# Routed experts of a six-stage network: new slots for the router's work, logits with both weight parts in one stationary operand, inverse roots by bits on VectorE, the next stage's statistics in the tail

## The chip, the cores and the metric

The kernel runs on one core of one Trainium2 chip. The metric is the time of one execution on the device in microseconds; the median of three runs is compared. Engines are named as in the profile: PE is TensorE, DVE is VectorE, ACT is ScalarE, POOL is GpSimd, SP is SyncE.

## The reference, cut to what matters

The network has six stages on `x` of (4, 1024, 256), 4096 tokens of 256 numbers:

```python
x = x + 0.5 * ffn0(layernorm(x))      # call 0: routed experts
x = x + attn0(layernorm(x))           # call 1
x = x + 0.5 * ffn0(layernorm(x))      # call 2: the same experts again
x = x + 0.5 * ffn1(layernorm(x))      # call 3
x = x + attn1(layernorm(x))           # call 4
x = x + 0.5 * ffn1(layernorm(x))      # call 5
```

The routed experts, `ffn0`, are:

```python
h = layernorm(x) * g + b              # of the normalised x: two norms in a row
logits = h @ Wr                       # (4096, 7)
top_vals, top_idx = top_k(logits, 2); gates = softmax(top_vals)
pos = place of each (token, choice) in its expert, in order; keep = pos < 732
xe[expert, pos] = h[token]
ye = (silu(xe @ W1) * (xe @ W3)) @ W2           # per expert, 256 -> 1024 -> 256
routed[token] += gate * keep * ye[expert, pos]
shared = (silu(h @ W1s) * (h @ W3s)) @ W2s      # every token
out = routed + shared
```

732 is the capacity of an expert (`CAP0`).

## The kernel before, in words

`x` stays in SBUF as `X`, 32 tiles of 128 tokens. Each stage is a class (`Ffn0`, `Attn0`, `Ffn1`, `Attn1`) with one ordered list of items. Every engine goes through the same list and issues what it has to do of each item (methods `pe`, `act`, `dve`, `pool`, `sp`), so the list sets the order on each queue, and semaphores carry what depends on what. Between stages stands a barrier, the item `meet`.

**A routed call (`Ffn0`).** Each product is made in three matmuls of fp32r parts (`mm3`, lines 160 to 162): high x high, low x high, high x low. The shared FFN of all tokens is `units` 0 to 3 of 8 steps each; unit 3 has one of its two halves here and the other at the very end. The seven experts are the units between. A step `s` is: `up(s, h)` for each half `h` (two banks of 12 matmuls altogether, Silu on ACT at line 502, product on DVE at 587, high part on ACT at 506, low part on DVE at 590), then `down(s - 1)`, and in every other step the load `ld` (SP, lines 860 to 862) and the split `wt` of the next weights (ACT 512, DVE 595). All shared steps work on banks 0 to 2 and 4 to 7; the router's work shares bank 3 and one buffer `AUX`.

**The router's work is put into slots** between the pieces of the first 24 steps, three slots to a step: slot `3s` is behind `up(s, 0)`, `3s + 1` behind `up(s, 1)`, `3s + 2` at the step's end. The items are: `stats` (mean and variance of tiles, lines 177 and 180), `root` (inverse root of the variance), `norm` (line 214, writes the normalised tiles `Z`), `tp(h, c)` (four transposes of a group of 512 tokens at line 457, gain and bias on ACT at 535, high part at 545, low part on DVE at 621), `lg(h)` (logits of 512 tokens, eight matmuls at line 474, read by ACT at 551), `lt(h)` (four small transposes of them at 481, copied by DVE at 626), `best` (the two largest of each token, 632 and 636), `tot` (one-hot table at 640 and 644, totals over all tokens at 484, a copy at 650), `pos` (method `positions`, the row number of each token and choice, with Exp on ACT for the gates), and `scat` (GpSimd, line 794).

Before, tiles 0 to 7 get all of this ahead of step 0, one part in a row, and the split of the first weights is last. Groups 2 to 7 have `tp` from slots 13, 17, ... 33; `tot` is in slot 38, `pos` in 39.

**The scatter.** 64 indirect DMAs write rows of 272 numbers of `Z` to memory `xe_scratch`, 32 for each choice; column 256 is the gate, 257 the token. Behind the first 32, GpSimd waits for them to land (the item `("scat", n, 4)`), copies the second choice's gate into column 256 (line 791) and issues the other 32. It then reads the rows of experts 0 and 1 (`xr`, line 804). TensorE asks for expert 0's rows in unit 3 of the shared FFN (`xt`, line 464), in step 26:

```python
elif ui == 3 and 2 <= j < 6:
    sl[2] = [("xt", n, 0, j - 2)] + ([("gi", n, 0)] if j == 5 else [])
```

**The roots.** `Ffn0.root` makes two roots in a row, as there are two norms: `Sqrt` on ACT (line 518), then a reciprocal and a Newton step on DVE, twice; the variance of the second norm is worked out from the first. The other stages take `Ln` and `Exp` on ACT (lines 209 and 211) and two Newton steps of four DVE instructions each (lines 197 to 203). ACT holds one set of tables at a time: Silu, Sqrt and Exp each need a load (`ACT_TABLE_LOAD`).

**Tails.** In the last unit `xget` reads X back from memory, since the experts' results were added there; the last sums into X are at line 661. Then `meet`, then the next stage begins with its statistics.

Of the kernel before, what the change touches and what calls it, by code (L numbers as in the profile page):

```python
# [16 lines left out]
LOW, HIGH = 16512, 229344  # L17

# [78 lines left out]
class Chip:  # L97
# [4 lines left out]
    def __init__(self, nc, A, out, ctx):  # L102
# [9 lines left out]
        self.S1, self.S2, self.S3, self.S4 = (self.sm(NT) for _ in range(4))  # L112
# [70 lines left out]
    def root_var(self, e, w, gs):  # L183
        w.wait_ge(*self.p.mine())
        e.tensor_scalar(self.S1[:, gs], self.MV[:, gs, 1], 1e-5, None, ALU.add).then_inc(*self.p.one("ln_var"))

    def root_dve(self, e, w, gs, it, by=None):
# [4 lines left out]
        if not by:  # L192
            self.root_var(e, w, gs)
        w.wait_ge(*p.at("ln_root", by or it))
        for n in range(2):
            i_ = o if n else s2
            e.tensor_tensor(s3, i_, i_, ALU.mult).then_inc(*p.one("dv"))
# [3 lines left out]
            e.tensor_scalar(s3, s3, -0.5, 1.5, ALU.mult, ALU.add).then_inc(*p.one("dv"))  # L201
            w.wait_ge(*p.mine())
            e.tensor_tensor(o, i_, s3, ALU.mult).then_inc(*p.one("rt" if n else "dv"))
            w.wait_ge(*p.mine())

    def root_act(self, e, w, gs, it, by=None):
        p = self.p
        w.wait_ge(*p.at("ln_var", by or it))
        e.activation(self.S2[:, gs], self.S1[:, gs], ACT.Ln).then_inc(*p.one("ac"))
        w.wait_ge(*p.mine())  # L210
        e.activation(self.S2[:, gs], self.S2[:, gs], ACT.Exp, scale=-0.5).then_inc(*p.one("ln_root"))
# [20 lines left out]
class Ffn0:  # L232
# [9 lines left out]
        "root": {}, "norm": {"z": 1},  # L242
# [7 lines left out]
    def __init__(self, chip, call, first):  # L250
# [23 lines left out]
        self.GI, self.IF6 = [c.sm(6) for k in range(2)], c.sm(12)  # L274
# [20 lines left out]
        for it in self.items:  # L295
# [3 lines left out]
            if it[0] == "root" and it[3] < 2:  # L299
                counts = {"ln_var": 1, "ln_root": 1}  # L300
# [10 lines left out]
            p.count(it, counts)  # L311
        c.back = {b: (self.back(2 * b), ("xget", call, min(2 * b + 1, 6))) for b in range(4)}
# [3069 lines left out]
```

## Time and profile before

| what | us |
|---|---|
| median of three runs | 3152.45 (3150.3 to 3153.19) |
| the profiled execution's own time | 3148.64 |
| its span | 3146.8 |
| PE busy | 2809.8 (89%) |
| DVE busy | 1821.0 (58%) |
| ACT busy | 1644.4 (52%) |
| POOL busy | 610.2 (19%) |

The profiled execution's own time is 1.84 us over its span. Times in rows are us from the span's start; the clock is the share of 2.4 GHz that was granted to PE, so 0.50 is the lower level of 1.2 GHz. Call 0 goes from 0 to 738 us, the first attention to 1107, call 2 to 1831. Matmuls overlap, so a busy PE is not a PE at its peak.

### The profile page before, as it was taken

The page shows a single profiled execution, that of the slowest core. Times are in us where ns is not written, and L with a number is a line of the kernel's source. Part 1 is how long each engine was busy: PE and PEld are TensorE (multiplying, and loading weights), DVE is VectorE, ACT ScalarE, POOL GpSimd, SP SyncE. Part 2 cuts the span into 40 slices and gives each one's busy share as a digit, 9 for nine tenths or more (in the row PEclk, how much of TensorE's full clock was granted, in tenths as well). Part 3 has the DMA queues.
Part 4 walks back from the last instruction along what each step waited for, and adds up shares of the span by engine and source line. Part 5 has one row for each costly group of instructions (what it writes and reads, how often), then busy time and mean ns, then how long its engine had stood idle before and what let it go on. Part 6 is the DMA issues. An engine that isn't in the chain of part 4 may idle for free.

```text
span 3146.8 us, 53051 instructions
## 1 busy us (share of the span) xinstructions
PE 2809.8 (89%) x21463; PEld 2169.0 (69%) x21463; DVE 1821.0 (58%) x3719; ACT 1644.4 (52%) x2535; POOL 610.2 (19%) x555
## 2 busy tenths in 40 slices
PE   6898999997999968989999945897899999993998
PEld 4677999995666656779999935796333434332898
DVE  5554555546777665545555467786635364326786
ACT  3433455543443434335555433564687778891665
POOL 0026021212000000360212254633000000001343
PEclk9999999998999989999999977998999999995999
DMA  3224243323000021232433344574442243413675
GB/s 130 89 69 131 87 100 83 85 70 87 2 2 2 2 51 44 90 121 78 100 81 94 77 133 130 152 196 109 101 121 46 65 105 96 80 34 115 169 192 129
DMA packets 240643, 287.20 MB, mean 91 GB/s; under 512 B 30916, under 2 KB 218492, under 8 KB 240400
## 3 DMA queue, kind: packets, MB, share of 16 engines
q1 hardware_dynamic: 201856, 223.88, 24.8%
q0 software_dynamic: 34848, 56.28, 9.0%
q8 instruction: 169, 2.77, 0.4%
q10 hardware_dynamic: 3696, 3.67, 0.4%
q14 instruction: 74, 0.61, 0.1%
HBM read 204.72 MB, written 87.93 MB: 93 GB/s over the span
## 4 chain that ended last, share of the span: by engine, by line
PE 63%; DVE 12%; issue 8%; POOL 7%; ACT 5%; DMA 4%; SPq 0%; POOLq 0%; DVEq 0%; ACTq 0%
PE PS L2842 14%; PE PS L160 12%; PE PS L161 11%; PE PS L162 11%; PE PS L1001 9%; POOL xe_scratch L794 4%; POOL xa_scratch L2295 1%; ACT FW L512 1%; PE PS L474 1%; DVE SM L177 1%; DVE FW L595 1%; DMA GR<-xn_scratch,SM 1%; POOL GR L2280 1%; ACT Z L561 1%; DVE PROD L587 1%
## 5 line engine op out<-in xcount | busy, mean ns | idle before, releaser
L2991 ACT ACTIVATE P<-PS 128x1024 f32<-128x1024 f32 x512 | 487.9, 1035 | 106.4 <-PE PS L2842 104.1
L160 PE MATMUL PS<-FH,FW 128*128 128x366 f32 (+1 forms) x1408 | 512.7, 364 | 26.4 <-DVE FW L595 13.5
L161 PE MATMUL PS<-FH,FW 128*128 128x366 f32 (+1 forms) x1408 | 502.9, 357 | 0.0
L162 PE MATMUL PS<-FH,FW 128*128 128x366 f32 (+1 forms) x1408 | 499.9, 355 | 0.0
L506 ACT ACTIVATE FHH<-PROD 128x366 fp32r<-128x366 f32 (+1 forms) x352 | 195.3, 555 | 487.0 <-DVE PROD L587 487.0
L160 PE MATMUL PS<-FW,FHH 128*122 128x256 f32 (+1 forms) x1184 | 339.4, 287 | 1.5 <-DVE FHH L590 1.5
L587 DVE TENSOR_TENSOR PROD<-SIL,PS 128x366 f32<-128x366 f32 (+1 forms) x352 | 207.0, 588 | 226.1 <-PE PS L162 215.6
L590 DVE TENSOR_TENSOR FHH<-PROD,FHH 128x366 fp32r<-128x366 f32 (+1 forms) x352 | 210.0, 596 | 218.6 <-ACT FHH L506 218.6
L161 PE MATMUL PS<-FW,FHH 128*122 128x256 f32 (+1 forms) x1184 | 335.3, 283 | 0.0
L162 PE MATMUL PS<-FW,FHH 128*122 128x256 f32 (+1 forms) x1184 | 334.5, 283 | 0.0
L160 PEld LDWEIGHTS PS<-FH,FW 128*128 128x128 f32 x1408 | 268.4, 191 | 54.8 <-ACT SIL L502 14.8
L162 PEld LDWEIGHTS PS<-FH,FW 128*128 128x128 f32 x1408 | 269.5, 191 | 22.7
L161 PEld LDWEIGHTS PS<-FH,FW 128*128 128x128 f32 x1408 | 268.2, 191 | 19.5 <-issue 1.5
L2842 PE MATMUL PS<-P,V 128*32 128x512 f32 x2048 | 273.3, 606 | 1.9 <-DVE OC L3138 1.4
L812 POOL DMA_INDIRECT xa_scratch<-Z,SM x84 | 140.9, 1677 | 615.1 <-ACT Z L561 593.7
L595 DVE TENSOR_TENSOR FW<-WST,FW 128x1536 fp32r<-128x1536 f32 x96 | 168.7, 1757 | 148.1 <-ACT FW L512 148.1
L502 ACT ACTIVATE SIL<-PS 128x366 f32<-128x366 f32 (+1 forms) x352 | 180.9, 514 | 127.8 <-PE PS L162 127.2
L794 POOL DMA_INDIRECT xe_scratch<-Z,SM x128 | 146.9, 1148 | 440.9 <-DVE SM L760 401.5
L160 PEld LDWEIGHTS PS<-FW,FHH 128*122 128x122 f32 (+1 forms) x1184 | 222.9, 188 | 5.7 <-DVE FHH L590 1.9
L161 PEld LDWEIGHTS PS<-FW,FHH 128*122 128x122 f32 (+1 forms) x1184 | 222.8, 188 | 2.7
L162 PEld LDWEIGHTS PS<-FW,FHH 128*122 128x122 f32 (+1 forms) x1184 | 222.6, 188 | 0.0
L2842 PE MATMUL PS<-S,S 64*128 64x512 f32 x1024 | 195.2, 454 | 1.4 <-DVE S L3132 1.0
(446 smaller groups left out, 5446.4 us busy)
## 6 DMA issues: line engine op xcount, KB each, us to landing
WS<-L_ffn_w_dram SPq DMA_DIRECT2D x256, 256.0 KB, 3.8
WST<-L_ffn_W_dram SPq DMA_DIRECT2D x168, 256.0 KB, 3.6
S<-parts_scratch SPq DMA_DIRECT2D x60, 384.0 KB, 7.9
parts_scratch<-PT SPq DMA_DIRECT2D x28, 512.0 KB, 4.4
Z<-xe_scratch POOLq DMA_DIRECT2D x14, 777.8 KB, 8.5
WST<-L_ffn_W1s_dram SPq DMA_DIRECT2D x40, 256.0 KB, 2.9
WST<-L_ffn_W3s_dram SPq DMA_DIRECT2D x40, 256.0 KB, 3.6
WST<-L_ffn_W2s_dram SPq DMA_DIRECT2D x40, 256.0 KB, 4.2
```

Of the source, the lines that this page charges most:

```text
L160: e.matmul(o, lh, rh, start=start, stop=False, skip_group_check=True)
L161: e.matmul(o, ll, rh, start=False, stop=False, skip_group_check=True)
L162: return e.matmul(o, lh, rl, start=False, stop=stop, skip_group_check=True)
L502: e.activation(self.SIL[:, h, 0:NH], c.bank(2 * self.up_at[it] % 3, NH), ACT.Silu).then_inc(*p.one("sil"))
L506: e.activation(self.FHH[:, s % 2, 0, hs], self.PROD[:, h, 0:NH], ACT.Copy).then_inc(*p.one("hi"))
L587: e.tensor_tensor(self.PROD[:, h, 0:NH], self.SIL[:, h, 0:NH], c.bank((2 * self.up_at[it] + 1) % 3, NH), ALU.mult).then_inc(*p.one("mul"))
L590: e.tensor_tensor(self.FHH[:, s % 2, 1, hs], self.PROD[:, h, 0:NH], self.FHH[:, s % 2, 0, hs].bitcast(F32), ALU.subtract).then_inc(*p.one( ...
L595: e.tensor_tensor(self.FW[:, q % 2, 1, :], self.WST[:, q % 2, :], self.FW[:, q % 2, 0, :].bitcast(F32), ALU.subtract).then_inc(*p.one("wo"))
L794: e.indirect_dma_start(out=c.XE, out_offset=bass.IndirectOffsetOnAxis(ap=c.ROWS.bitcast(U32)[:, m:m + 1], axis=0), in_=self.Z[:, m % NT, : ...
L1001: mm = lambda o, l, r, a=True, z=True: e.matmul(o, l, r, start=a, stop=z, skip_group_check=True)
L2842: mm = lambda o, l, r, a=True, z=True: e.matmul(o, l, r, start=a, stop=z, skip_group_check=True)
L2991: e.activation(self.PR[K % 3][:, 2 * jj:2 * jj + 2, :].rearrange("p a b -> p (a b)"), c.pair(2 * ((2 * K + jj) % 3)), ACT.Exp, scale=0.25) ...
```

## The change

Slots: the split of the first weights (`wt 0`) goes ahead of the first transposes, and the split of the router's weights gets an item of its own (`wrr`) behind the norms, so that statistics wait for neither. The groups' `tp` begin at slots 7, 11, ... 27; the one-hot table becomes an item `oh` in slot 32, `tot` is in 33, `pos` in 34, `scat` in 35 to 42, the reads of rows in 44.

```diff
-        seq += [("stats", n, 0, 0, 4), ("stats", n, 0, 4, 8)] + [("root", n, 0, k) for k in range(3)]
-        seq += [("norm", n, i, i + 4) for i in (0, 4)] + [("tp", n, h, c) for h in range(2) for c in range(2)]
-        seq += [("wt", n, 0)]
+        self.ahead = [[("stats", n, 0, 4)], [("stats", n, 4, 8)]]
+        seq = [("consts", n), ("ld", n, 0), ("ld", n, 1), *self.ahead[0], *self.ahead[1], ("root", n, 0, 8)]
+        seq += [("norm", n, i, i + 4) for i in (0, 4)] + [("wrr", n), ("wt", n, 0)]
+        seq += [("tp", n, h, c) for h in range(2) for c in range(2)]
...
-            slots[k].append(it)
-        for k in range(8):
-            slots[k].append(("stats", n, 1 + 3 * k // 8, 8 + 3 * k, 11 + 3 * k))
-        for k in range(3):
-            slots[8 + k].append(("root", n, 1, k))
-        for k in range(12):
-            slots[11 + k].append(("norm", n, 8 + 2 * k, 10 + 2 * k))
+            slots[k + k // 4].append(it)
+        for k, a, b in ((0, 8, 11), (1, 11, 14), (2, 14, 16), (4, 16, 18), (5, 18, 20), (7, 20, 23), (8, 23, 26),
+                        (9, 26, 29), (10, 29, 32)):
+            slots[k].append(("stats", n, a, b))
+        slots[3].append(("root", n, 8, 16))
+        slots[11].append(("root", n, 16, 32))
         for h in range(2, 8):
-            s0 = 13 + 4 * (h - 2)
+            s0 = 7 + 4 * (h - 2)
+            for k in range(2):
+                slots[s0 - 3 + k].append(("norm", n, 4 * h + 2 * k, 4 * h + 2 * k + 2))
...
-        slots[38].append(("tot", n))
-        slots[39].append(("pos", n))
+        slots[32].append(("oh", n))
+        slots[33].append(("tot", n))
+        slots[34].append(("pos", n))
         for k in range(8):
-            slots[40 + k].append(("scat", n, k))
-        slots[48] += [("xr", n, 0), ("xr", n, 1), ("xput", n, 7)]
+            slots[35 + k].append(("scat", n, k))
+        slots[44] += [("xr", n, 0), ("xr", n, 1), ("xput", n, 7)]
```

Logits: the high and the low part of the router's weights stand side by side in one stationary operand of 16 columns, so a group takes four matmuls, and both halves are summed as they are read from the small transposes.

```diff
-                    for x, y in ((0, 0), (1, 0), (0, 1), (1, 1)):
-                        ins = e.matmul(pb[0:8, :], self.WRR[:, y, cc, :], self.FH[h // 2][:, x, cc, hs],
...
+                    for x in range(2):
+                        ins = e.matmul(pb[0:16, :], self.WRR[:, cc, :, :].rearrange("p y e -> p (y e)"),
+                                       self.FH[h // 2][:, x, cc, hs], start=cc + x == 0, stop=cc + x == 2,
...
-            e.tensor_copy(self.LG[:, 4 * h:4 * h + 4, 0:7],
-                          c.bank(3, 32).rearrange("p (i e) -> p i e", e=8)[:, :, 0:7]).then_inc(*p.one("ad"))
+            e.tensor_reduce(self.LG[:, 4 * h:4 * h + 4, 0:7],
+                            c.bank(3, 64).rearrange("p (i y e) -> p i e y", y=2, e=8)[:, :, 0:7, :], AX,
+                            ALU.add).then_inc(*p.one("ad"))
```

Roots: one function for all stages, twelve DVE instructions, none on ACT. The first guess comes from the number's bits; the double norm of `Ffn0` is one root of `v * (1 + eps) + eps * eps`. In the second attention the items `rv` and `ra` go, and the shift of one `root` stands for them.

```diff
+    def root(self, e, w, gs, done, by=1.0, more=EPS):
...
+        e.tensor_scalar(s1, self.MV[:, gs, 1], by, more, ALU.mult, ALU.add).then_inc(*p.one("dv"))
...
+        e.tensor_scalar(s2, s1.bitcast(U32), -0.5, 1597463007.0, ALU.mult, ALU.add).then_inc(*p.one("dv"))
...
+        e.tensor_copy(o.bitcast(U32), s2).then_inc(*p.one("dv"))
...
+        for n in range(3):
+            e.scalar_tensor_tensor(s3, o, -0.5, o, ALU.mult, ALU.mult).then_inc(*p.one("dv"))
...
             e.tensor_tensor(s3, s3, s1, ALU.mult).then_inc(*p.one("dv"))
...
+            e.scalar_tensor_tensor(o, s3, 1.5, o, ALU.add, ALU.mult).then_inc(*p.one(done if n == 2 else "dv"))
```

Scatter: the row carries both gates and the token's first expert (columns 256, 258, 259), and the reader takes the gate that belongs to its expert: four DVE instructions in `gi` for two. The wait and the copy between the two halves go.

```diff
-            if it[2] == 4:
-                w.wait_ge(*p.at("scat", ("scat", n, 3)))
-                w.wait_ge(*p.mine())
-                e.tensor_copy(self.Z[:, :, D], c.GT[:, 1, :]).then_inc(*p.one("po"))
-                w.wait_ge(*p.mine())
...
+        e.tensor_copy(self.Z[:, :, D + 2], c.GT[:, 1, :]).then_inc(*p.one("dv"))
+        e.tensor_copy(self.Z[:, :, D + 3], self.IF[:, 0, :]).then_inc(*p.one("dv"))
```

Tails: `joined` moves a stage's first items into the list of the stage before. A routed call takes the first attention's two pairs of statistics ahead of its last `up`, and their root ahead of its last sums; the first attention takes call 2's two pieces of statistics ahead of `("lc", 1, 3, 0, 0)` and `("le", 1, 3, 3)`, near its end. `Ffn1` and `Attn1` neither give nor take.

```diff
+def joined(ph, after):
+
+    pieces = after.ahead if after and ph.rooms else ()
+    out, at = [], 0
+    for room, piece in zip(ph.rooms, pieces):
+        out += [(ph, ph.items[at:room]), (after, piece)]
+        at = room
+    out.append((ph, ph.items[at:]))
...
+        self.rooms = [self.items.index(it) for it in (self.ups[-1], ("xs", call, len(self.units) - 1))]
...
+        self.ahead = [self.items[1:3], self.items[3:4]]
+        self.rooms = [self.items.index(("lc", call, 3, 0, 0)), self.items.index(("le", call, 3, 3))]
```

## Rows read from the trace of the kernel before

**Rows 1.** The chain that ended last, its summary by line (share of the span).

```profile
by line: PE PS L2842 13.7%; PE PS L160 12.1%; PE PS L161 11.3%; PE PS L162 11.3%; PE PS L1001 8.9%; issue 8.2%; POOL xe_scratch L794 3.7%; POOL xa_scratch L2295 1.3%; ACT FW L512 1.1%; PE PS L474 1.0%; DVE SM L177 1.0%; DVE FW L595 0.9%; DM
```

**Rows 2.** Windows, call 0: stretch, length, busy us (x instructions) per engine, PEclk, DMA share, GB/s.

```profile
28.50:77.50 49.00, 43.91 (x212) 35.08 (x213) 30.94 (x109) 19.73 (x27) 0.00 (x0) 0.92 0.23 79
77.50:189.20 111.70, 98.09 (x533) 76.54 (x532) 56.18 (x158) 47.33 (x70) 0.00 (x0) 0.94 0.21 71
189.20:209.10 19.90, 15.57 (x65) 11.91 (x66) 12.62 (x36) 4.89 (x7) 0.00 (x1) 0.83 0.21 66
209.10:303.70 94.60, 94.60 (x550) 83.61 (x550) 46.28 (x60) 35.73 (x53) 72.13 (x64) 1.00 0.35 115
```

**Rows 3.** The same view, call 2; engines in the order PE, PEld, DVE, ACT, POOL.

```profile
1131.00:1180.00 49.00, 43.94 (x213) 35.11 (x214) 31.03 (x110) 19.73 (x27) 0.00 (x0) 0.92 0.22 49
1180.00:1286.00 106.00, 93.67 (x533) 74.65 (x531) 56.42 (x158) 47.32 (x70) 0.00 (x0) 0.98 0.13 40
1286.00:1305.00 19.00, 15.07 (x66) 11.64 (x67) 12.21 (x36) 5.01 (x7) 0.21 (x1) 0.91 0.22 71
1305.00:1400.00 95.00, 94.91 (x552) 83.79 (x550) 46.39 (x61) 36.03 (x53) 73.27 (x65) 1.00 0.35 117
1400.00:1412.50 12.50, 0.14 (x1) 0.17 (x2) 2.35 (x2) 1.48 (x1) 1.24 (x3) 0.57 0.84 232
```

**Rows 4.** Waits of PE, 0 to 720 us: us in total, times, longest.

```profile
PE PS L464 <- DMA Z<-xe_scratch: 13.7, 1, 13.7
PE PS L474 <- DVE FH L621: 8.4, 6, 3.2
...
PE PS L160 <- ACT SIL L502: 5.1, 7, 2.9
PE PS L484 <- DVE RT L644: 4.6, 1, 4.6
```

**Rows 5.** Timeline, start of call 0: start us, us, instruction, idle before.

```profile
9.71 1.40 DVE L177 BATCH_NORM_STATS2 SM<-X 128x6 f32<-128x256 f32 x4
...
13.49 0.17 DVE L710 TENSOR_SCALAR SM<-SM 128x8 f32<-128x8 f32 x1
...
17.22 2.80 DVE L214 TENSOR_SCALAR Z<-X,SM 128x256 f32<-128x256 f32 x8
...
28.52 0.80 PE L160 MATMUL PS<-FH,FW 128*128 128x512 f32 x1 [6.12 <-DVE FW L595]
```

**Rows 6.** DMA issues of 0 to 4.7 us: KB each, median us to landing.

```profile
X<-L_attn_x_dram SPq DMA_DIRECT2D x1, 512.0 KB, 5.0
...
WST<-L_ffn_W2s_dram SPq DMA_DIRECT2D x1, 256.0 KB, 9.8
```

**Rows 7.** Call 2: DMA issues of 1107 to 1110.2 us; then the timeline's first matmul.

```profile
WST<-L_ffn_W2s_dram SPq DMA_DIRECT2D x1, 256.0 KB, 4.4
...
1130.97 0.80 PE L160 MATMUL PS<-FH,FW 128*128 128x512 f32 x1 [6.12 <-DVE FW L595]
```

**Rows 8.** Groups of instructions (busy us, mean ns, idle before), from call 0.

```profile
L474 PE MATMUL PS<-FH,WRR 128*8 128x512 f32 x64 | 19.0, 446 | 10.6 <-DVE FH L621 8.4 <-DVE RT L626 2.1
...
L457 PE MATMUL PS<-IDENT,Z 128*128 128x128 f32 x64 | 11.2, 316 | 22.3 <-DVE Z L214 20.6 <-DVE RT L626 1.7
...
L791 POOL COPY Z<-SM 128x32 f32<-128x32 f32 x1 | 0.2, 243 | 3.1 <-DMA xe_scratch<-Z,SM 3.1
```

**Rows 9.** Groups of instructions, call 0: loads of ACT's tables ahead of Sqrt.

```profile
L518 ACT ACT_TABLE_LOAD x3 | 3.8, 1283 | 9.7 <-issue 9.7
```

**Rows 10.** Timeline, inside the scatter of call 0, DVE and POOL.

```profile
249.76 1.76 DVE L595 TENSOR_TENSOR FW<-WST,FW 128x1536 fp32r<-128x1536 f32 x1 [2.38 <-ACT FW L512]
...
249.84 2.54 POOL L794 DMA_INDIRECT xe_scratch<-Z,SM  x1 [0.30 <-issue]
```

**Rows 11.** Timeline, end of call 0 and start of the attention, DVE.

```profile
736.81 1.29 DVE L661 SCALAR_TENSOR_TENSOR X<-PS,X 128x512 f32<-128x512 f32 x2 [1.79 <-PE PS L162]
...
742.96 0.75 DVE L177 BATCH_NORM_STATS2 SM<-X 128x6 f32<-128x256 f32 x2
```

More of the change, by code:

```diff
@@ L17 @@
 LOW, HIGH = 16512, 229344
+EPS = 1e-5
 class Sig:
@@ L111, in __init__ @@
         self.ST, self.MV, self.R = self.sm(8, 6), self.sm(NT, 2), self.sm(NT)
-        self.S1, self.S2, self.S3, self.S4 = (self.sm(NT) for _ in range(4))
+        self.S1, self.S2, self.S3 = (self.sm(NT) for _ in range(3))
         self.GB = self.sm(2, 2)
@@ L273, in __init__ @@
         self.OUT = c.sm(2)
-        self.GI, self.IF6 = [c.sm(6) for k in range(2)], c.sm(12)
+        self.GI, self.G2, self.IF6 = [c.sm(6) for k in range(2)], c.sm(6), c.sm(12)
         self.IU = [self.IF6[:, 6 * k:6 * k + 6].bitcast(U32) for k in range(2)]
@@ L512, in act @@
             e.activation(self.FW[:, q % 2, 0, :], self.WST[:, q % 2, :], ACT.Copy).then_inc(*p.one("wh"))
-        elif k == "root":
-            g, part = it[2:]
-            if part < 2:
-                gs = slice(8, NT) if g else slice(0, 8)
-                w.wait_ge(*p.at("ln_var", it))
-                e.activation(c.S2[:, gs], c.S1[:, gs], ACT.Sqrt).then_inc(*p.one("ln_root"))
         elif k in ("tp", "xt"):
@@ L1579, in act @@
         kk = 16 * len(self.bs)
-        if k == "root" and not self.apart:
-            c.root_act(e, w, self.columns(it), it)
-        elif k == "ra":
-            c.root_act(e, w, self.columns(it), it, ("rv", *it[1:]))
-        elif k == "sk" and it[3] == 0:
+        if k == "sk" and it[3] == 0:
             s = it[4]
@@ L1611, in dve @@
         elif k == "root":
-            c.root_dve(e, w, self.columns(it), it, self.apart and ("ra", *it[1:]))
-        elif k == "rv":
-            c.root_var(e, w, self.columns(it))
+            c.root(e, w, self.columns(it), "rt")
         elif k == "zn":
@@ L1937 @@
     NW = 64
+    ahead, rooms = (), ()
     CONSTS1 = 7, 11, 15, 19, 20, 21, 22, 23, 24
@@ L2634, in prep @@
             q.add(1, ("stats", n, "p", b, i), ("stats", n, "p", b, i + 1))
-        for delay, k in ((1, "rv"), (2, "ra"), (2, "root")):
-            q.add(delay, (k, n, "p", b))
-        q.add(1, ("zz", n, b, 0))
+        q.add(1, ("root", n, "p", b))
+        q.add(5, ("zz", n, b, 0))
         q.add(1, ("zz", n, b, 1), ("xb", n, b))
@@ L2682, in sink_jobs @@
         last = b == 2
-        for delay, k in ((1, "rv"), (2 - last, "ra"), (2 - last, "root")):
-            q.add(delay, (k, n, b, 0))
+        q.add(1, ("root", n, b, 0))
         job = []
@@ L3288, in sp @@
             self.all_loaded(w)
+def joined(ph, after):
[5 more added lines that the diff above has]
+    out.append((ph, ph.items[at:]))
+    if pieces:
+        moved = {it for piece in pieces for it in piece}
+        after.items = [it for it in after.items if it not in moved]
+    return out
 KINDS = [Ffn0, Attn0, Ffn0, Ffn1, Attn1, Ffn1]
```

129 lines of the change are left out of this document (44 added, 85 removed), and 6 rows, old and new, of the table COUNTS.

## The prediction

> **What bounds the kernel now.** The chain that ended last comes first: five lines of matmuls hold 57% of it, and the scatter of tokens to the experts (line 794), which computes nothing, holds 3.7% by itself [rows 1]. So the stage that scatters is cut into stretches. In both calls the same picture: a start; four steps of the shared FFN; a long router part; a short stretch up to the moment when the row numbers are ready; 95 us in which TensorE is full at a granted clock of 1.00 while GpSimd scatters; and a hole, 12.5 us long in call 2, in which it does nothing [rows 2, 3]. The waits of TensorE in call 0 put the hole at 13.7 us, all of it for the scattered rows, and show three more kinds: 8.4 us in six waits for the halves of the transposed tokens, 4.6 us in one for the one-hot table, and 2.9 us in the longest of those for ScalarE's Silu [rows 4]. In the shared steps the profile's clock is under 1.00, so time is lost there at the lower of the two levels (1.2 GHz) as well.
>
> **The start of each call.** Before, the first shared matmul issues at 28.52, because the weight split stands behind all four transposes on ScalarE and VectorE [rows 5]. Now the split stands ahead of them, and the statistics no longer wait for gate and bias. The last third of the weights is issued at 4.2, near the end of a stretch of 4.7 us, and lands 9.8 later, at 14.0; the first eighth of X, issued with the first DMAs at 0.8, lands 5.0 later, at 5.8 [rows 6]. Statistics of eight tiles took 3.8 us; the root's 17 small instructions 3.73, 0.22 each [rows 5], so twelve take 2.6; the norms 2.8: normalised tiles are ready at 15.0, beside the weights' copy (14.0 to 15.5) and subtraction (to 17.3). Two subtractions of transposed halves follow, taken as 0.8 each (a third of the weights' 1.76 for a third of the columns is 0.6, the rest for ScalarE's copy): first matmul at 18.9, 9.6 us earlier. In call 2 the statistics are already done in the attention's tail; the weights, issued at 1109.8, land 4.4 later, at 1114.2 [rows 7], and the same 5 us behind them give 1119.2 for 1130.97: 11.8 us. Bounds: 6 and 13 us, as the landing of the weights moves.
>
> **Logits.** Line 474 took 19.0 us for 64 matmuls, 8 per group [rows 8], 2.4 us a group with those at the lower clock; I take 2.0 at the full one. Half of them go, 1.0 us per group. That a stationary of 16 columns costs more than one of 8 is not in the trace; weight loads there lie beside matmuls of 512 columns, so nothing to 0.1 us each, and I take nothing. The summing read of 16 columns in place of a copy I bound by 0 and 0.3 us per group and take nothing: VectorE only, beside TensorE's next matmuls.
>
> **The first four steps** (slots 0 to 11). TensorE was busy 43.9 of 49.0 us [rows 2]. The new slots put in a third logits group (1.0), three transposes (11.2 us for 16 groups, 0.7 each [rows 8]) and 0.4 for a small transpose, less 2 x 1.0 for the halved groups: +1.5. They bring one more wait of 8.4/6 = 1.4. The 2.9 us wait goes: it stands behind the switch of tables from Sqrt back to Silu (1283 ns a switch [rows 9]), and with it about 1.7 of the 3.9 us that a clock of 0.92 lost. 49.0 + 1.5 + 1.4 - 2.9 - 1.7 = 47.3. VectorE is near the same: 30.9 busy, plus 1.5 for two roots, 2.2 for three pairs of norms and 2.1 for three subtractions is 37, plus 0.7 of idleness behind each of eight products: 43. So little is won here, and bounds are -4 and +6 us.
>
> **The router part** (slots 12 to 37 before, 12 to 31 now). Of 98.1 us busy, 6.7 were lost to a clock of 0.94 and 6.0 go with the logits: 85.4. Twelve transposes, six logits groups, six small ones hold 16.8 of it, so a shared step costs 68.6 / 8.67 = 7.9. Now there are 6.67 steps (52.8) with nine, five and five of those (13.3): 66.1. Idle was 13.6; I keep it by slots, 10.5, and 5 for the clock: 81.6 for 111.7. In call 2 the same with 12.3 idle and a clock of 0.98: 66.1 + 9.5 + 2 = 77.6 for 106.0 [rows 3].
>
> **Up to the row numbers.** 19.9 us before. The one-hot table is now made a slot ahead of the totals, so the 4.6 us go, with the 3.4 that a clock of 0.83 lost; one more half step of 2.6 lies in it. 14.5; in call 2, 19.0 - 4.6 - 1.7 + 2.6 = 15.3. The two added copies (0.2 each) are inside the bound.
>
> **The scatter.** The row numbers come 5 slots, 1 2/3 steps, earlier against TensorE's work, so TensorE now has 94.6 + 1.67 x 7.9 = 107.8 us to do before it asks for the first expert's rows. From the same moment the rows took 94.6 + 13.7 = 108.3 to land; 4.1 of it (3.1 of landing, 0.2 of copy [rows 8], and 0.8 until the next issue) was the second gate's column, which goes: 104.2. So the hole closes with 3.6 us to spare. In call 2 it is 95.0 + 13.2 = 108.2 against 107.5 less 3.1 (a shorter landing by 1), 104.4. That margin is all that hides the scatter; a lack is paid one for one. On GpSimd's queue only the two reads of rows stand behind the 64 issues.
> A scatter issue of 0.98 us took 2.54 when a 1.76 us VectorE subtraction began beside it [rows 10]. The Trainium skill ("SBUF — State Buffer", Who interferes with whom) says the shared port pair is an exclusive lock and its loser blocks; the trace agrees, and by it the scatter's time depends on how many subtractions fall into it. By the rows six do, now as before: the sum stays.
>
> **Sum of the calls.** Call 0: 49.0 + 111.7 + 19.9 + 94.6 + 13.7 = 288.9 before, from the first matmul on; 47.3 + 81.6 + 14.5 + 107.8 = 251.2 now; 37.7 gained, and 9.6. Call 2: 281.5 against 47.3 + 77.6 + 15.3 + 108.2 = 248.4; 33.1, and 11.8. Together 92.2 us. What the clock gives back behind the hole is not counted.
>
> **The tails and the other roots.** Between the last sum into X (ended 738.10) and the third pair's statistics lie 4.86 us [rows 11]; less a barrier, taken as 0.2, 4.7 go. In the tail of the call VectorE idled 1.79 us before that sum; the root of 2.6 fits it but for 0.8. The statistics ahead of it need X's first blocks back from memory; if they are late, the last product waits behind them (bounds 0 and 4). In the attention's own tail two pieces of statistics stand ahead of products and sums: 0 if VectorE waits there anyway, 3.8 if all lies on the path; its last sums wait for TensorE, so I take 0. Two roots at the second attention's start cost 0.2 each more. There the set of tables holds both Ln and Exp, so the roots by bits take no table switch away: that part of the change gains nothing outside the routed calls. 4.7 - 0.8 - 0.4 = 3.5.
> By "ScalarE: Activation LUTs" of the Trainium skill (Table sets) a switch costs about 2.7 us; the trace has 1.283 [rows 9], and the measurement decides. With 2.7 the removed wait would be worth 2.8 us more per call.
>
> **Total.** 92.2 + 3.5 = 95.7 us. The profiled execution took 3148.64, so 3052.9; it stands 3.8 us under the median of the runs (3152.45), so the median should be 3057.
>
> **Rivals.** A: the scatter still ends last. TensorE reaches the rows with only 3.6 us of margin; three collisions more, at 1.5 us each, or a faster router part after the row numbers, bring back 1 to 8 us per call with the clock's fall behind it. For it: the margin is 3% of the stretch. Against: both sides are counted from the same moment. 3057 + 12 = 3069. Chance 0.16.
> B: VectorE bounds the dense slots. Its 43 us of 47 are in order, and each wait of it delays a product that TensorE's next banks need. If the first steps take 6 us more than before and the router part keeps its old pace per slot of 4.3 us (86 for 81.6), each call loses (6 + 1.7) + 4.4 = 12.1 of its gain: 3081. For it: the 43 us counted above. Against: the slots before were filled by half as much and TensorE waited 5 us in 49. Chance 0.18.
> C: slower than before. The clock: it fell wherever TensorE paused. If short pauses now come in every slot and hold it at 1.2 GHz, a step of 7.9 us takes up to 15.8. It decides from the point where 96 us of such work, 12 of the 21 steps up to the row numbers in both calls, runs low; if all 21 do, it loses 166 and the time is 3223. Against: the same work has 0.92 to 0.98 [rows 2, 3]. Chance 0.02.
> D: the slots' order is not what sets the pace, and start and hole are all that comes: 21.4 + 26.2 = 48; 3105. Chance 0.03.
> By "TensorE: Matmul & The Clock Gate" of the Trainium skill (The HAM clock gate), the clock is one of two levels and follows how busy TensorE has been; the trace agrees (the hole's mean is 0.57 [rows 3]), and this is the page beside C.
>
> **How the numbers follow.** Forecast 0.60; A 0.16, B 0.18, D 0.03, C 0.02, no change 0.01. The unknown terms (start 6 to 13, first steps +-5, router part +-8 per call) add to about +-25 round 3057; the range reaches to B on the slow side: 3030 to 3090. About 0.2% (6 us) is what a measurement of this kernel can tell from no change: faster 0.97, same 0.01, slower 0.02.
>
> **What would show it.** First shared matmul near 19 us, and 12 us behind the second routed call's start; line 474 with half its matmuls; no table load for Sqrt; first scatter near 162 us after the start, the 64 issues in one piece of about 92 us; no wait of TensorE for the expert rows; the attention's first transposes 4 us earlier behind the last sum. It would be wrong if a wait for rows of over 5 us stands, if VectorE's busy share in the first four steps nears 1, or if the clock there falls under 0.85.

## The result, and the profile after

The changed kernel took 3069.58 us (median of 4 runs, 3065.97 to 3079.62), the kernel before beside it 3151.38 (3147.87 to 3153.19): a ratio of 0.9747 (0.972 to 0.9773), 82 us less. Forecast were 3057, within 3030 to 3090, and a gain of 95.7. The profiled execution is the slowest of the four, 3079.62 us with a span of 3077.7, 69.1 less than the span of 3146.8 before. Where a difference of some microseconds matters, the second profile of the same kernel (changed_again, below; span 3065.0, 81.8 less) stands beside it.

The windows of the changed kernel, cut at the first shared matmul, the start of the fifth step, the first scatter and the first transposes of the experts' rows. ([rows 2, 3] have their second border 4.5 us later, inside the fifth step; the section on the prediction comes back to this.) Busy us and instructions of PE, PEld, DVE, ACT, POOL; then clock, DMA share, GB/s:

```profile
19.06:66.61 47.55, 39.97 (x204) 31.54 (x205) 35.75 (x120) 19.66 (x29) 0.00 (x0) 0.96 0.24 83
66.61:182.08 115.47, 94.39 (x508) 76.70 (x507) 61.54 (x188) 44.44 (x66) 0.00 (x0) 0.91 0.22 73
182.10:289.00 106.90, 106.90 (x622) 94.55 (x621) 51.99 (x67) 40.96 (x60) 74.83 (x66) 1.00 0.41 130
1095.05:1144.67 49.62, 43.00 (x205) 33.54 (x205) 35.84 (x120) 19.71 (x29) 0.00 (x0) 0.87 0.28 49
1144.67:1240.49 95.82, 88.98 (x508) 73.01 (x507) 61.46 (x188) 44.16 (x66) 0.00 (x1) 1.00 0.14 45
1240.50:1347.50 107.00, 107.00 (x622) 94.59 (x621) 52.07 (x67) 41.00 (x60) 76.19 (x66) 1.00 0.41 128
```

There is no fourth stretch any more: TensorE is full from the first scatter to the experts' rows in both calls, and the holes of 13.7 and 12.5 us are gone. But the middle stretch, router part and row numbers together, takes 115.5 us in call 0 and 95.8 in call 2, for the same work; TensorE idles 21.1 us in the one and 6.8 in the other. Its waits in call 0 say on what (0 to 720 us; total, times, longest):

```profile
PE PS L449 <- DVE Z L205: 14.5, 2, 13.4
PE PS L466 <- DVE FH L609: 11.6, 6, 6.8
PE PS L449 <- DVE RT L614: 11.6, 3, 9.7
...
PE PS L477 <- DVE RT L633: 1.9, 1, 1.9
```

The first is the start. The wait for the one-hot table fell from 4.6 to 1.9, and none is left for the experts' rows [rows 4]. Two single waits are new, 6.8 and 9.7 us. VectorE, named in both, was itself idle ahead of them, in its weight splits, here the sixth (VectorE's timeline):

```profile
140.55 1.76 DVE L583 TENSOR_TENSOR FW<-WST,FW 128x1536 fp32r<-128x1536 f32 x1 [8.29 <-ACT FW L505]
```

Before, the sixth split stood at 140.73: the same moment, though TensorE had started 9.5 us later. What holds it stands on SP's queue (timeline; start, us, issues that ran one behind the other):

```profile
75.29 15.32 SPq L821 DMA_DIRECT2D WST<-L_ffn_W1s_dram  x1
...
95.81 13.04 SPq L795 DMA_DIRECT2D xe_scratch<-RT  x2
108.89 11.34 SPq L821 DMA_DIRECT2D WST<-L_ffn_W1s_dram  x1
120.28 7.04 SPq L822 DMA_DIRECT2D WST<-L_ffn_W3s_dram  x1
```

L795 writes zeros into the experts' scratch, 777.8 KB at a time from 122 partitions, seven times in call 0 and never in call 2; a weight load whose issue takes 0.4 us elsewhere waits 11 and 15 behind it. From 98 to 106 us, where these writes run with no more than the rest of one weight load beside them, the DMA share is 0.13, two engines of 16, at 49 GB/s. So the theory to be tested was: in call 0 the pace is that of SP's queue. Its rivals: the denser slots of VectorE, or the clock (0.91 in that stretch).

Three more readings. The start and the seam between call 0 and the attention came as forecast (first shared matmul; last sum of call 0, statistics, norm):

```profile
19.06 0.77 PE L161 MATMUL PS<-FH,FW 128*128 128x512 f32 x1 [2.02 <-DVE FH L609]
```

```profile
706.10 1.29 DVE L651 SCALAR_TENSOR_TENSOR X<-PS,X 128x512 f32<-128x512 f32 x2
707.53 0.76 DVE L178 BATCH_NORM_STATS2 SM<-X 128x6 f32<-128x256 f32 x2
708.32 0.25 DVE L181 BATCH_NORM_AGGREGATE SM<-SM 128x2 f32<-128x6 f32 x2
708.60 1.88 DVE L205 TENSOR_SCALAR ZBUF<-X,SM 128x256 f32<-128x256 f32 x4
```

From sum to norm it is 2.50 us where it was 7.22. But from that norm to the barrier of call 2 the attention took 375.3 us where it had taken 363.1 (744.03 to 1107.13): it lost 12. A part of that is a fall of the clock some 300 us behind the norm. In all profiles of this study it stands in five of the ten with statistics in this stage's tail and in none of the four without (windows, changed kernel):

```profile
1010.00:1015.00 5.00, 5.00 (x82) 4.55 (x76) 1.47 (x5) 2.11 (x3) 0.00 (x0) 0.50 0.00 0
1015.00:1020.00 5.00, 5.00 (x36) 1.42 (x34) 1.31 (x2) 1.55 (x3) 0.00 (x0) 0.58 0.02 3
```

The rest was the second thing to be tested: statistics for call 2 now stand in the attention's tail, its last piece behind the last sum into X.

### The profile page after: what moved, and what is told of

Same layout as the page of the kernel before. It is cut to its first block, busy times and chain, and to the rows that moved or that the text cites. A ratio compares the mean times of both kernels' runs of the same rounds, so it can differ in the third digit from the quotient of the medians.

```text
span 3077.7 us, 52954 instructions
## 1 busy us (share of the span) xinstructions
PE 2793.7 (91%) x21399; PEld 2162.1 (70%) x21399; DVE 1832.4 (60%) x3808; ACT 1625.3 (53%) x2488; POOL 611.7 (20%) x553
## 4 chain that ended last, share of the span: by engine, by line
PE 70%; DVE 12%; issue 6%; POOL 3%; ACT 3%; DMA 3%; SPq 2%; DVEq 0%; POOLq 0%; ACTq 0%
PE PS L161 15%; PE PS L2795 14%; PE PS L162 14%; PE PS L163 14%; PE PS L964 9%; POOL xa_scratch L2249 1%; DVE SM L178 1%; ACT FW L505 1%; DMA WST<-L_ffn_W2s_dram 1%; DMA GR<-xn_scratch,SM 1%; SPq L821 1%; ACT Z L548 1%; POOL GR L2234 1%; DVE FW L583 1%; PE PS L456 1%
## 6 DMA issues: line engine op xcount, KB each, us to landing
Z<-xe_scratch POOLq DMA_DIRECT2D x14, 777.8 KB, 7.8
```

## The experiments

The runs fell on three chips. On chip 7 the kernel before took 3148.68 us; on chip 6 3236.94 to 3237.8 and on chip 13 3236.99, since TensorE on these two stands still for nothing that the profile names while GpSimd scatters (last section; the expectations call it waiting for its own instructions). The record names no chip for the first measurement; its times and traces are like those of chip 7. Every ratio is to the kernel before, run beside it on the same chip, and times are compared within a chip only. Up to a call's first scatter the chips agree: where the code is the same, it comes at 182.54 on chip 6 and at 182.50 on chip 7 in call 0, and 144.9 and 145.0 us behind the first shared matmul in call 2. So these moments are compared across chips. In call 2 this distance differs by itself: with the same router work it is 143.0 to 146.2 us in six profiles.

**Zeros on 16 engines**, the test of the queue:

```diff
-e.dma_start(c.XE[e_ * CAP0:(e_ + 1) * CAP0, :].rearrange("(p a t) d -> p a (t d)", a=2, t=3),
-            self.ZERO[0:122].unsqueeze(1).broadcast_to([122, 2, 3 * ROW]))
+e.dma_start(c.XE[720 * e_:720 * e_ + 720, :].rearrange("(p a t) d -> p a (t d)", a=3, t=3),
+            self.ZERO[0:80].unsqueeze(1).broadcast_to([80, 3, 3 * ROW]))
+if e_ == 6:
+    e.dma_start(c.XE[5040:5124, :], self.ZERO[0:84, 0:ROW])
```

> The changed kernel, with the seven zero writes of the experts' scratch cut so that each starts from 80 partitions (720 rows) instead of 122, and 84 rows written by one small transfer behind the last. Theory Q (queue): call 0 misses its forecast (first scatter 182.1 instead of 162) because the zero writes take 13 to 16 us each on SP's queue at some 50 GB/s and the next weights stand behind them; spread wider they take 3 to 5 us, the sixth weight split starts before 130 instead of at 140.6, the first scatter comes at 162 to 168, and the time falls by 14 to 20 us to about 3053. Rival V (VectorE's dense slots or the clock set the pace of call 0): the weight splits do not move by more than 2 us and the time is within 4 us of 3070.

> The kernel before, with the same wider zero writes. Theory Q: the queue stood in the way there too, but the slots left more room; its router part took 5.7 us longer in call 0 than in call 2 (111.7 for 106.0), so it gains 4 to 8 us, to about 3145, clearly less than the changed kernel does. Rival Q2 (the queue costs the same in either order of slots): it gains as much as the changed kernel, 14 us or more. Rival V: nothing, within 3 us of 3151.

Measured on chip 6: 3181.84 us, ratio 0.9824 (0.9807 to 0.9842). The sixth split and the first scatter (timelines of VectorE and GpSimd):

```profile
126.14 1.75 DVE L585 TENSOR_TENSOR FW<-WST,FW 128x1536 fp32r<-128x1536 f32 x1
```

```profile
164.81 1.16 POOL L757 DMA_INDIRECT xe_scratch<-Z,SM  x1 [161.00 <-DVE SM L728]
```

14.4 and 17.3 us earlier than in the changed kernel, as the theory of the queue had it. VectorE no longer idles ahead of the split, and the weights' issues on SP's queue take 0.4 us again. The kernel before with the same edit took 3235.44, ratio 0.9982 (0.9961 to 1.0003), its first scatter at 205.89 for 209.10: 3.2 us. So the queue cost 3 us in the old order and 17 in the new one: its pace had lain just behind TensorE's, and the change ran into it. The absolute 3053 could not show on that chip.

**Zeros on ScalarE's queue**, narrow as they were, to tell the order on the queue from the width. The edit moves the issue of L795 from SP's stream to ScalarE's.

> The changed kernel with the narrow zero writes (122 partitions) as they are, but issued by ScalarE on its own queue. Theory O (order on the queue is what counts): the weights no longer stand behind them, the sixth split comes at 124 to 128 instead of 140.6, and the time is about 3067 - 16 = 3051. Rival E (their two DMA engines are what counts; the weights' packets on those two wait for them whatever the queue): the sixth split stays within 4 us of 140.6, the time at 3062 to 3069.

3203.74 us on chip 6, ratio 0.9895 (0.9875 to 0.9915). The sixth split stood at 144.99, the first scatter at 183.68: nothing is won. But the reason is another one. ScalarE copies the weights ahead of each split; its waits from 30 to 184 us (total, times, longest) had this line in the changed kernel, and have none for weights in this one:

```profile
ACT FW L505 <- DMA WST<-L_ffn_W2s_dram: 17.5, 2, 10.9
```

In its place stands this one:

```profile
ACT SIL L495 <- issue: 20.4, 3, 9.0
```

ScalarE's timeline shows what it stood behind, its own issues of the zero writes:

```profile
73.85 9.58 ACTq L542 DMA_DIRECT2D xe_scratch<-RT  x1
...
93.14 7.53 ACTq L542 DMA_DIRECT2D xe_scratch<-RT  x1
...
111.95 4.98 ACTq L542 DMA_DIRECT2D xe_scratch<-RT  x1
```

So rival E's forecast was nearly met (the split came 4.4 us later, not within 4), but its reason, weights that wait whatever the queue, is not in the trace. Theory O had the reason right, the weights are in time again, and left out what the issue costs an engine that computes: a narrow write holds up the stream that issues it. Its width is what counts on either queue: from 80 partitions the same issues took 0.6 us each on SP's. "DMA: Bandwidth & Descriptors" of the Trainium skill has a rule for the width and one for the queues: a transfer takes the largest number of engines up to 16 that divides its slowest dimension (Why a DMA increments its semaphore by 16 and not by 1), which for 122 partitions is 2, for 80 is 16; and transfers issued by different engines end up on the same 16 and interleave (Issuing engines are not separate DMA queues). With the first the traces agree, with a share of 0.13. The second no run here shows by itself: ScalarE never had to wait for the weights, and no view tells how their packets fared beside the zeros.

**The changed kernel again**, with three others on chip 7:

> The changed kernel itself, unaltered, beside the others of this call. In the runs so far it took 0.9747 of the kernel before (0.972 to 0.9773). If TensorE again waits for its own instructions while GpSimd scatters (118 to 128 us of such waits in the last four kernels, 1.3 in the first profile of before), the ratio moves: theory H (the waits last as long as the issues of the scatter, in either kernel) gives 3237.8 - 82 = 3156 to 3237.8, about 0.975 to 0.988, since the hole that the change closes is then covered by another stall. Against the first call's kernel with zeros on 16 engines (0.9824) theory Q says this one is 14 to 20 us slower, 0.987 to 0.989.

3067.27 us (3066.83 to 3072.6), ratio 0.9751 (0.9735 to 0.9767): the first measurement, repeated. Those standstills were not there (2.0 us), so of theory H this run says nothing.

**The scatter in two pieces**, new slots kept:

```diff
+if it[2] == 4:
+    w.wait_ge(*p.at("scat", ("scat", n, 3)))
+    w.wait_ge(*p.mine())
+    e.tensor_copy(self.Z[:, :, D], c.GT[:, 1, :]).then_inc(*p.one("po"))
+    w.wait_ge(*p.mine())
```

(and the two added columns and their use in `gi` taken out).

> The changed kernel with the scatter as it was: after 32 issues a wait for the landing and a copy of the second gate, and 32 more; the rows carry one gate. Theory S (a slack of 4 us): in the profile of the changed kernel the rows of the first expert land 4.9 us before TensorE asks for them in call 0 and 3.5 before in call 2; the column costs 4.1, so the holes stay under 1 us each and the time rises by 0 to 2 us: the new slots alone close the hole. Rival P (the piece is needed): collisions and the fall of the clock behind a short hole make it 4 to 12 us.

3069.09 us, 1.8 more than the changed kernel and within the range of its runs (3066.83 to 3072.6), ratio 0.9752 (0.9736 to 0.9768); no wait of TensorE for rows. They were issued at 279.80 and landed 7.9 later, at 287.7; TensorE asked at 289.89. Theory S: the new slots close the hole, and the one piece only widened a slack that was already enough.

**Eight logits matmuls** of 8 columns per group, with the copy in place of the summing read:

```diff
-for x in range(2):
-    ins = e.matmul(pb[0:16, :], self.WRR[:, cc, :, :].rearrange("p y e -> p (y e)"), ...
+for x, y in ((0, 0), (1, 0), (0, 1), (1, 1)):
+    ins = e.matmul(pb[0:8, :], self.WRR[:, cc, y, :], ...
```

> The changed kernel with eight logits matmuls of 8 stationary columns per group in place of four of 16, and a copy in place of the summing read. Theory L: 1.0 us more for each of the 16 groups, of which call 0's part past the fourth step is hidden while its weights are late: 16 at most, 10 at least; about +13 us. Rival M (logits lie in TensorE's waits, beside VectorE's work): under 5 us.

3073.53 us, 6.3 more, ratio 0.9768 (0.9751 to 0.9784): between the two expectations. The groups of logits matmuls, 0 to 720 us, first of this kernel, then of the changed one run beside it (busy us, mean ns | idle before):

```profile
L466 PE MATMUL PS<-FH,WRR 128*8 128x512 f32 x64 | 17.7, 423 | 11.3 <-DVE FH L609 9.1 <-DVE RT L614 2.1
```

```profile
L466 PE MATMUL PS<-FH,WRR 128*16 128x512 f32 x32 | 10.8, 468 | 13.1 <-DVE FH L609 11.0 <-DVE RT L614 2.1
```

TensorE is spared 6.9 us a call, near the 8 of the price. In call 0 none of it reaches the path: the first scatter is at 181.52 with eight and at 182.50 with four, since the weights set the pace. In call 2, from first shared matmul to first scatter, it is 149.9 for 145.0: 4.9 us, and still 3.7 more than the longest of the six profiles with halved logits. The halved logits are worth about 5 us in this kernel, not 16.

**No statistics in the tails** (`pieces = ()` in `joined`), and **one tail only** (`rooms = ()` for the first attention, together with the wide zeros):

> The changed kernel with the next stage's statistics no longer put into the tail of the stage ahead. Theory T (they are free in the tails): 4.0 us more at the attention's start (two pairs of statistics and what lies around them) and 2 to 4 more at the second routed call's start, where the landing of the weights hides part of it: 3070 + 7 = 3077. Rival W (they delay products in the attention's tail, part of why the first attention took 375.3 us behind its norm where it took 363.1 before): the attention gets back up to 12 us, and the time is 3058 to 3070.

3198.95 us on chip 6, ratio 0.9881 (0.9861 to 0.9902). End of the attention in VectorE's timeline, first of the changed kernel, then of this one (last sum into X, then the first instruction behind the barrier):

```profile
1081.16 0.69 DVE L1394 TENSOR_TENSOR X<-X,PS 128x512 f32<-128x512 f32 x1 [1.04 <-PE PS L964]
1081.89 1.41 DVE L178 BATCH_NORM_STATS2 SM<-X 128x6 f32<-128x256 f32 x4
1083.33 0.38 DVE L181 BATCH_NORM_AGGREGATE SM<-SM 128x2 f32<-128x6 f32 x4
1083.88 0.07 DVE L560 MEMSET SM<- 128x16 f32 x1 [0.17 <-DVEq L3191]
```

```profile
1143.06 0.69 DVE L1394 TENSOR_TENSOR X<-X,PS 128x512 f32<-128x512 f32 x1 [1.04 <-PE PS L964]
1143.92 0.07 DVE L560 MEMSET SM<- 128x16 f32 x1 [0.17 <-DVEq L3191]
```

1.9 us of the second piece lie open behind the last sum. The first piece costs too. From the same ScalarE copy (L1203, the second of its last four; the next expectation calls it the last) to the barrier it is 16.7 us with the statistics and 13.5 without: 3.2, of which 1.3 arise in front of the last sum. There VectorE's products follow one another without a pause, the first piece stands among them, and TensorE waits for VectorE (TensorE's timelines, changed kernel, then this one):

```profile
1071.71 1.07 PE L964 MATMUL PS<-E,ZB 128*32 128x512 f32 x8 [1.89 <-DVE RY L1387]
```

```profile
1133.29 1.06 PE L964 MATMUL PS<-E,ZB 128*32 128x512 f32 x8 [0.27 <-ACT E L1194]
```

Norm to barrier took 363.1 and 363.3 us in the two profiles of kernels before, 365.5 here, all else new, and in the ten profiles with statistics 367.4 to 370.1 without the fall of the clock and 371.1 to 375.3 with it. The seam behind call 0 behaves as expected: 7.32 us from sum to norm without, 2.50 with. At the start of call 2 the statistics are of little use, since the weights land late anyway: from barrier to first shared matmul 12.81 us without, 11.17 to 13.22 with.

> The changed kernel with the wide zero writes and without the statistics in the attention's tail (those in the first routed call's tail stay). Theory T2: in the traces of the last call the attention's end took 16.7 us from its last ScalarE copy on with these statistics and 13.5 without, and the routed call behind it started its shared matmuls 12.8 us after its barrier without them and 11.2 to 12.4 with: so they cost 1.6 to 2.7 net, and this kernel is 2 us faster than with wide zeros alone, 16 to 22 under the changed kernel. Rival T1 (they pay): it is 2 to 4 us slower than with wide zeros alone, 12 to 16 under the changed kernel.

3045.19 us on chip 7 (3042.19 to 3049.56), ratio 0.9676 (0.966 to 0.9692): 22.1 under the changed kernel beside it, the upper end of theory T2. The first scatter is at 163.92, the last sum of call 0 at 688.03 for 706.63 (18.6 us), and norm to barrier took 365.5 for 370.1. Wide zeros alone were not run on this chip, so the total cannot tell T2 from T1; the parts speak for T2, since the attention gives back 1.9 to 4.6 us against the profiles with statistics and without the fall, and the start of call 2 takes 0.6 more than beside it. This is the best kernel of the study, 103 us under the kernel before.

**Roots by ScalarE** in the routed calls: the Sqrt of 8 to 16 tiles, a reciprocal and a Newton step in place of `c.root`:

```diff
+e.tensor_scalar(s1, c.MV[:, gs, 1], 1.0 + EPS, EPS * EPS, ALU.mult, ALU.add).then_inc(*p.one("lnv"))
+w.wait_ge(*p.at("lnr", it))
+e.reciprocal(o, s2).then_inc(*p.one("dv"))
...
+e.activation(c.S2[:, gs], c.S1[:, gs], ACT.Sqrt).then_inc(*p.one("lnr"))
```

> The changed kernel with the roots of the routed calls by ScalarE's Sqrt, a reciprocal and one Newton step, three roots a call at the same places. Theory A: each root in a slot brings two switches of ScalarE's tables of 1.283 us and a wait of VectorE for ScalarE; I costed such a wait at 2.9 us and 1.7 for the clock behind it, once per call; with two roots in slots, 5 to 9 us a call, but in call 0 the one in slot 11 is hidden by the late weights: 3067 + 10 to 16 = 3077 to 3083. Rival B2: they lie beside other work, 3067 to 3071.

3199.36 us on chip 6, ratio 0.9886 (0.9865 to 0.9906), between the neighbours there. The first scatter came at 182.84 (182.50 with roots by bits), and in call 2 it was 146.2 us behind the first shared matmul (145.0), although ScalarE's table loads are back. Rival B2: 0.3 and 1.2 us, and in call 2 this is inside the range of 143.0 to 146.2. Taking the table switches away gained next to nothing in the routed calls.

**The old slots**, all else new (the edit puts the slot table of before back, with `("root", n, 8, 32)` in slot 10):

> The changed kernel with the slots of the router's work as they were before (statistics in eight pieces, norms from slot 11, the first group of the router part at slot 13, totals at 38, scatter from 40, rows at 48), and all else new: the start, the halved logits, the roots by bits, one piece of scatter, statistics in the tails. By my terms the slots are worth 21.0 us in call 0 and 17.4 in call 2 (holes of 9.6 and 9.4 that come back, the late one-hot table, 26 slots of router work for 20). Theory Q: in call 0 SP's queue takes most of that away, so the old slots cost 2 to 6 there and 17 in call 2, in sum about 21: 3091. Rival V: the slots bring what I said in both calls and call 0 lost its 17 us elsewhere: 38 us, 3108. Rival N: the slots bring little anywhere, under 10 us: 3079 or less.

> The old slots in the changed kernel once more, since in the first call TensorE's waits for its own instructions covered the stretch in which they should show. Theory Q2 (corrected): the slots behind the held-up weight split count in full. First scatter 22 us later in call 0 (204.98 for 182.5 in the last trace) and 16 later in call 2, holes of 5 to 10 us behind them instead of none; less the TensorE work that then lies behind the hole instead of in front (5 slots, 13.2 us, in either call), so about 9 + 9 from the holes and their clock and 9 + 3 from the router part: 3067 + 20 to 30 = 3087 to 3097. Rival N: only the holes count, 3067 + 8 to 16.

> The old slots in the changed kernel, a third time, for a chip on which TensorE does not wait for its own instructions. From the two traces where it did: first scatter 22.1 us later in call 0 (204.6 for 182.5), and in call 2 164.5 us behind the first shared matmul instead of 145.0, 19.5 later. Behind it the changed kernel's TensorE has 106.9 and 107.1 us of work, of which 13.2 now lie in front of the scatter: 93.7 and 93.9, against 102.1 and 103.5 until the rows have landed: holes of 8.4 and 9.6. Theory S2: 22.1 - 13.2 + 8.4 = 17.3 and 19.5 - 13.2 + 9.6 = 15.9, in sum 33: 3067 + 33 = 3100 where the kernel before takes 3150 (ratio 0.984). Rival N (as on the other chip, where the ratio was 0.992 for about 0.988 of the changed kernel): the holes cost, the rest is covered: 3067 + 10 to 18, ratio 0.977 to 0.980. If TensorE's waits for instructions are there again, the ratio is 0.991 to 0.993 and nothing is learned of the holes.

3207.61, 3211.87 and 3214.8 us, ratios 0.9905 (0.9886 to 0.9923), 0.9921 (0.9901 to 0.994) and 0.9932 (0.991 to 0.9954), twice on chip 6 and once on chip 13. That is 8.7 us more than the kernel without statistics in the tails, run beside the first, and 12.5 more than the one with roots by Sqrt, run beside the second. What can be read on any chip is the way to the first scatter: 204.60 to 204.98 in call 0 for 182.50, 161.9 to 164.5 us behind the first shared matmul in call 2 for 145.0. The slots bring the scatter 22 and 17 to 20 us forward. My first expectation, that the queue takes most of this away in call 0, was wrong, and the second right: what the queue holds up is the sixth split (at 140.6 to 140.8 with the old slots, 140.6 and 140.7 with the new), which stands ahead of slot 26, and from there to the first scatter it is 9 slots now and was 14. What the holes then cost, and with that the worth of the slots in full, 33 us by my working, stays open: it has to be measured where TensorE does not stand still during the scatter, and no such run of the old slots exists.

## Why the prediction was right, and where it was not

It goes by the second profile of the changed kernel, whose span is 81.8 under that of before. By parts, forecast and measured (us gained):

| part | forecast | measured |
|---|---|---|
| call 0 up to its last sum | 47.3 - 0.8 | 30.2 |
| from there to the attention's norm | 4.7 | 4.7 |
| attention, norm to barrier | 0 | -7.0 |
| call 2, barrier to first matmul | 11.8 | 11.7 |
| call 2, from there to its last sum | 33.1 | 30.8 |
| the three stages behind | -0.4 | 11.4 |
| sum | 95.7 | 81.8 |

**The start** held: 19.06 us for 18.9, and 12.2 us behind the barrier of call 2 for 12.

**The first four steps** took longer than before, not shorter, and a border in the wrong place hid it. The prediction lets them end at 77.5 and 1180 us, but in the kernel before the fifth step's first matmul is at 73.00 and 1175.42; the 49.0 us of [rows 2, 3] hold 20 of its matmuls, which fill 4.5 us. The four steps by themselves, of the kernel before in both calls, then of the changed kernel with the old slots in call 0:

```profile
28.52:73.00 44.48, 39.41 (x192) 31.34 (x193) 27.73 (x99) 18.36 (x25) 0.00 (x0) 0.91 0.24 82
1130.97:1175.42 44.45, 39.39 (x192) 31.36 (x193) 27.72 (x99) 18.37 (x25) 0.00 (x0) 0.91 0.24 54
```

```profile
18.95:56.55 37.60, 34.85 (x184) 28.65 (x185) 28.03 (x94) 16.25 (x24) 0.00 (x0) 0.95 0.20 73
```

So the working gives 47.3 - 4.5 = 42.8 us, and it was 47.6 and 49.6 in the first profile, 48.3 and 47.6 in the second. The term that was too small is "one more wait of 8.4/6 = 1.4": in call 0 of the first profile four waits came, 5.3 us together. One of 0.3 is for ScalarE; the others, for VectorE's transposed halves, summing read and norms, are (19.1 to 66.61 us):

```profile
PE PS L466 <- DVE FH L609: 2.5, 1, 2.5
...
PE PS L449 <- DVE RT L614: 1.4, 1, 1.4
PE PS L449 <- DVE Z L205: 1.1, 1, 1.1
```

The new slots' own price in these steps is about 11 us (36.3 to 39.0 in call 0 with the old ones, 47.6 to 49.7 with the new), where the working has 4.9 (1.5, the 2.0 that it takes off for the halved logits, and the wait of 1.4). VectorE was busy 35.8 of 47.6 us, so it did not bound these steps as a whole, but rival B's reason was at work in them; its second half, a router part at the old pace, did not come. And the reason I gave for the wait that went fell: with Sqrt and its table switches back, the four steps took 48.6 and 48.0 us, so the switch by itself is not what cost there.

**Router part and row numbers** is where the step failed in call 0. "Idle was 13.6; I keep it by slots, 10.5" gave 96.1 us with the row numbers, 100.6 with the 4.5 that belong here; call 0 took 115.5, with TensorE idle for 21.1. Idle time does not shrink with the slots when what is waited for has a clock of its own. The zero writes on SP's queue stand in the trace of before in full length, with the sixth split at the end of them; I did not read that queue. With them widened, the same stretch takes 97.4 us (66.5 to 163.9), and in call 2, where there are none, it took 95.8 and 97.4 where the working gives 97.4. From the first shared matmul to the first scatter call 0 took 163.4 us for the 143.4 of the working, and 145.1 with the wide zeros: the queue is 18.3 of the 20. In call 2 it was 145.0 for 140.2, and that is the dense first steps.

**The scatter**: the margin of 3.6 us was right. The rows landed 4.9 us before TensorE asked in call 0 and 3.5 in call 2 (1336.12 and 7.9 against 1347.54), and 107 us of work lie in the stretch for 107.8 and 108.2. Rival A did not come; that the column's 4.1 us were needed was not true with these slots.

**Logits**: the price per matmul was near (6.9 us for 8 a call), the share on the path was not (about 0 and 5).

**The tails**: the first was exact. For the attention's tail I wrote "its last sums wait for TensorE, so I take 0" and left 3.8 as the bound; it cost 3.2, 1.9 for the piece behind the last sum and 1.3 for the one in front. Of the other 3.8 of the 7 us, 2.4 are there without any statistics in the tail (365.5 for 363.1), for no reason that a run shows; the remaining 1.4 is less than the profiles without the fall of the clock differ among themselves (367.4 to 370.1), and this profile is one of them.

**The other roots** were off to the good side. "That part of the change gains nothing outside the routed calls": at the second attention's start 2.38 us stand for 2.26, as forecast, but the three stages behind took 1305 to 1310 us in eleven profiles of the new roots and 1313.7 in the first one, where they had taken 1316.5 and 1315.6. All three stages have a part in it. Call 3, to its last load of X, took 345.0 and 346.8 us before and 342.0 to 345.3 in the new ones; from the issue of that load to call 5's first statistics it was 679.1 and 678.8, and 673.0 to 677.4 in those eleven; the rest took 295.3 and 293.3, and 290.8 to 292.4. That VectorE's roots no longer wait for ScalarE there is the likely cause; no run put the old ones back in those stages alone, so it is not shown.

So the time came within 13 us of the forecast by errors of opposite sign: 16 lost in call 0, which the wide zeros bring back, 7 in the attention and 2 in call 2, where the dense first steps cost 5, and 12 gained behind. That they cancelled to this degree is luck.

## What to carry to other kernels

Where a schedule is tightened by slots, list for each stretch what has its own pace (a DMA queue's issues, one by one, with their time) and when it would be done; the sum by slots holds only in front of that. A DMA queue that TensorE's waits never name can still be the next bound: here a weight split that stood at 140.7 and then at 140.6 gave it away, and an edit of six lines brought the end of call 0 forward by 18.6 us. Divide two kernels into stretches at the same instruction: 4.5 us at a border turned a loss into a gain here. And work put into a tail is free only where its engine would wait anyway: 1.9 us of statistics cost 1.3 among VectorE's unbroken products, and all of it behind the last sum.

## What was not expected of the hardware

On chips 6 and 13 TensorE stood still inside the scatters. Its waits for nothing that the profile shows ("issue") sum to 88 us in the kernel before with wide zeros and 106 to 116 in the kernels made from the changed one (the expectation of changed_again puts them at 118 to 128), for 1.3 to 2.8 in the first measurement's traces and on chip 7. From 190 to 210 us, first on chip 6 (zeros_on_16), then on chip 7 (changed_again), PE's busy time first:

```profile
190.00:200.00 10.00, 0.00 (x0) 0.00 (x0) 0.00 (x0) 0.00 (x0) 7.85 (x8) 0.50 0.30 108
200.00:210.00 10.00, 0.00 (x0) 0.00 (x0) 1.79 (x1) 1.48 (x1) 7.57 (x9) 0.50 0.42 140
```

```profile
190.00:200.00 10.00, 10.00 (x64) 9.04 (x63) 4.07 (x7) 3.09 (x5) 7.56 (x9) 1.00 0.64 228
200.00:210.00 10.00, 10.00 (x58) 8.79 (x57) 4.43 (x5) 3.72 (x5) 8.17 (x7) 1.00 0.50 172
```

VectorE and ScalarE stand still as well, with single waits of up to 44 us that the profile puts down to "remote" or "issue", while GpSimd issues its 64 scatters in 85 us (93 on chip 7); when they end, all go on. On chip 7 a packet of the DMA queue that the profile calls "q8 instruction" lands about every 20 us of this stretch; on chip 6 one lands at 187 us and then none up to 270. That fits instructions that come late, and it fits engines that ask for none because they stand for another reason; which it is, and why on two of the three chips, stays open. It matters for the change: more of TensorE's work now lies beside the scatter, so more of it is exposed. The changed kernel itself was not run there; its nearest kin (0.9881 to 0.9895) gain a little under half of what it gains on chip 7.
